# Rows of four edges, two to a partition, in the edge stage of a graph-and-mixer block

## The reference, cut to what matters

```python
xn = _layernorm(x)
e = einsum('ehd,ehd->eh', k[src], q[dst]) / 16        # 4 heads of 64
ex = exp(e - segment_max(e, dst)[dst])
a = ex / segment_sum(ex, dst)[dst]
ft2 = segment_sum(v[src] * a[..., None], dst)         # 3125 x 256
rst = layernorm(ft2 + xn); rst = layernorm(rst + ffn(rst))
x = x + rst + mixer(xn)
x = x + two_of_eight_experts(layernorm(x))
```

## Time and profile before

| | us |
|---|---|
| median of 3 runs | 2857.79 (2846.66 to 2863.58) |
| span of the profiled execution | 2291.0 |
| what lies around the span (median less span) | 566.8 |
| project stage | 0 to 118 |
| edge stage, with the second mixer | 118 to 1443 |
| merge stage | 1443 to 1585 |
| feed-forward part and experts | 1585 to 2291 |

### The profile page before, as it was taken

The page is one execution under the profiler, slowest core; times in us unless marked ns, Lnnn a source line. Parts: engine busy times, 40 slices in busy tenths (PEclk is TensorE's granted clock), DMA queues, the critical chain, the costliest instruction groups (busy, mean ns, idle before and its releaser), DMA issues. The chain is left out here.

```text
span 2291.0 us, 44322 instructions
## 1 busy us (share of the span) xinstructions
PE 1830.8 (80%) x12285; PEld 1291.9 (56%) x12285; DVE 1833.5 (80%) x3705; ACT 1525.4 (67%) x5228; POOL 1257.2 (55%) x1281
## 2 busy tenths in 40 slices
PE   7767788887786688787888771487999679999996
PEld 4433333333333566666666650244988579999995
DVE  7389999999999999999999999555899854444442
ACT  2267777778877587887888875687555255555553
POOL 0177777777777577777777776375000024444442
PEclk9879999889987688988989985698999789999998
DMA  8577777777777677777878787474001282222223
GB/s 229 182 230 232 231 230 235 233 224 228 228 226 228 182 230 239 235 234 237 237 232 242 226 243 211 138 206 119 15 29 32 89 280 38 35 35 36 37 37 77
DMA packets 213272, 394.34 MB, mean 172 GB/s; under 512 B 46354, under 2 KB 140637, under 8 KB 213005
## 3 DMA queue, kind: packets, MB, share of 16 engines
q0 software_dynamic: 91392, 278.99, 43.0%
q1 hardware_dynamic: 96848, 90.41, 13.3%
q10 hardware_dynamic: 24829, 22.64, 3.0%
HBM read 346.47 MB, written 48.65 MB: 172 GB/s over the span
## 5 line engine op out<-in xcount | busy, mean ns | idle before, releaser
L804 POOL DMA_INDIRECT ring<-kv_tab,idx x1008 | 981.0, 973 | 441.0 <-issue 297.6
L1132 ACT ACTIVATE act_val<-ring,act_val 128x64 f32<-128x64 f32 x2016 | 559.2, 398 | 51.0 <-DVE part L910 46.6
L855 DVE TENSOR_TENSOR prod<-ring,tile_bank 128x1024 f32<-128x1024 f32 x252 | 299.4, 1211 | 11.2 <-ACT tile_bank L1121 6.3
L862 DVE TENSOR_REDUCE score<-prod 128x16 f32<-128x1024 f32 x252 | 298.3, 1207 | 0.0
L2149 POOL DMA_INDIRECT x_sum<-e_yw,to_row x56 | 125.0, 2232 | 218.5 <-DVE e_yw L2175 197.2
L2134 POOL DMA_INDIRECT xr<-rows,from_row x56 | 57.6, 1029 | 291.2 <-issue 290.9
L2224 PE MATMUL e_h<-e_xT,e_now 128*128 128x128 f32 x1792 | 211.7, 277 | 0.8 <-DVE e_now L2165 0.8
L2224 PEld LDWEIGHTS e_h<-e_xT,e_now 128*128 128x128 f32 x1792 | 206.9, 194 | 1.3 <-DVE e_now L2165 1.2
L2239 PE MATMUL e_yps<-e_now,e_hT 128*128 128x256 f32 x896 | 202.5, 379 | 0.0
L2189 ACT ACTIVATE e_now<-e_w_all 128x2048 f32 x56 | 106.9, 1912 | 131.2 <-PE e_yps L2239 131.2
L2239 PEld LDWEIGHTS e_yps<-e_now,e_hT 128*128 128x128 f32 x896 | 166.2, 190 | 20.1
(11 more groups left out here) (425 smaller groups left out, 4794.0 us busy)
## 6 DMA issues: line engine op xcount, KB each, us to landing
loaded<-parts SPq DMA_DIRECT2D x150, 130.0 KB, 2.3
e_w_all<-L_ffn_W SPq DMA_DIRECT2D x16, 1024.0 KB, 12.2
parts<-part ACTq DMA_DIRECT2D x126, 130.0 KB
q_win<-q_tab SPq DMA_DIRECT2D x126, 128.0 KB
ring<-kv_tab,idx POOLq DMA_INDIRECT x1008
kv_tab<-kv_t SPq DMA_DIRECT2D x25, 224.0 KB
xn_buf<-x SPq DMA_DIRECT2D x25, 125.0 KB
x_sum<-x_buf SPq DMA_DIRECT2D x25, 125.0 KB
```

The lines of the kernel that those rows point to most:

```text
L804: pool.indirect_dma_start(out=ring[:, n % RING, e, :], out_offset=None, in_=t.kv_tab, in_offset=bass.IndirectOffsetOnAxis(ap=idx[n % 6][:, ...
L855: dve.tensor_tensor(prod[half][:, :, :], ring[:, n % RING, at, 0:F], bcast(q_ps[n % 2].unsqueeze(1), 128, L // 2, F), ALU.mult).then_inc(q ...
L862: dve.tensor_reduce(score[:, at, :], prod[half][:, :, :].rearrange("p s (h d) -> p s h d", h=HG), AX.X, ALU.add).then_inc(reduced, 1)
L1132: one = act.activation(act_val[n % 2][:, h, 0:DG, e - L // 2], ring[:, n % RING, e, F + h * DG:F + (h + 1) * DG], ACT.Copy, scale=act_val[ ...
```

## The change

A row now has 4 edges (`L` = 4) and a partition holds two rows (`G` = 2), so that a tile is 256 rows with the same 8 gathers of 128; `TILES` becomes 113 and `N_STEPS` 137. Row group 0 is weighed by DVE, group 1 by ACT. `times_q` multiplies in place, into the key half of `ring`. `weigh` of tile n-1 moves to the head of tile n, between the two `times_q`. ACT writes its weighted values beside DVE's, and the four additions become two of 1040 and 520 elements. `compare` has 256 columns and stands one step earlier; its form is now that of an operation on two tensors. Queries are fetched twice (one matmul and one load of 128 KB for each group), table rows too (four transfers per tile in place of two). Their PSUM buffers are single now. `find` and `settle` are cut in two. A sixteenth of the micro steps is doubled up (`micros`), since there are fewer tiles. In the mixer's key half the values' matmuls of two heads are issued next to each other, the products with ones are dropped, and their sums come from a product of the keys with themselves (`gram_sums`) instead. The merge loads 260 KB per step, scales one group on POOL and the other on DVE, makes one matrix on ACT and the other on DVE, and issues two matmuls per step.

```diff
-L = 8
+L = 4
+G = 2
-TILES = -(-(NB - 1 + N) // 128)
+TILES = -(-(NB - 1 + N) // (128 * G))
+EXTRA = 16
+def micros(n, c):
+    i = 4 * n + c
+    return range(i + i // EXTRA, i + 1 + (i + 1) // EXTRA)
...
 # POOL: gathers
-                for e in range(L):
+                for g in range(G):
+                    wait(pool, (val_ready, act_val_ready)[g], n - RING + 1)
+                    for e in range(L):
...
 # DVE, edge stage
+                dve.scalar_tensor_tensor(later[n % 2][:, :, :], place[:, :, :], float(128 * G * n),
+                                         bcast(blocks[n % NBUF][:, :, 2 * T3C:].bitcast(F32), 128, G, 128), ALU.add, ALU.is_ge)
...
+                k = ring[:, n % RING, g * L:(g + 1) * L, 0:F]
+                dve.tensor_tensor(k, k, bcast(q_ps[g].unsqueeze(1), 128, L, F), ALU.mult).then_inc(q_read[g], 1)
...
             def fold(n):
                 dve.wait_ge(val_ready, n + 1)
-                dve.wait_ge(exp_ready, n + 1)
-                dve.tensor_tensor(v[:, 0:2, :], v[:, 0:2, :], v[:, 2:4, :], ALU.add).then_inc(folding, 1)
+                dve.wait_ge(act_val_ready, n + 1)
+                dve.tensor_tensor(v[:, :, 0:2 * FD], v[:, :, 0:2 * FD], v[:, :, 2 * FD:], ALU.add).then_inc(folding, 1)
...
+                dve.tensor_tensor(part[n % 2][:, :, :], v[:, :, 0:FD], v[:, :, FD:2 * FD], ALU.add).then_inc(folded, 1)
...
-            def sum_act(n):
-            def fold_last(n):
...
 # DVE's order in tile n: times_q 0, weigh n-1, times_q 1, add_up 0 and 1, keep_own, compare n+5, top, less_top, fold n-1, fold_on n-1
...
 # PE
+            def q_of_rows(n, g):
+                wait(pe, q_read[g], n)
+                if g == 0:
+                    wait(pe, val_ready, n - 1)
+                pe.matmul(q_ps[g], spread[n % NBUF][:, g, :], q_win[n % 2][:, g, :], start=True, stop=True)
...
-                    pe.matmul(normT_ps[beyond, :], one_col[:, 1 - half:1 - half + DM], phi_k[h % 2], ...)
+                        for head in (h, h + 1):
+                            pe.matmul(gT_ps[half][at, :], v1[u % 2][:, head, 1:V1], phi_k[head % 2], ...)
...
 # merge
             for n in range(N_STEPS):
-                pe.matmul(step_ps[n % 3][:, 0:FD], hot[n % 4][:, :], scaled[n % 3][:, :], start=True, stop=True)
+                pe.matmul(step_ps[n % 3][:, 0:FD], hot0[n % 4][:, :], scaled0[n % 3][:, :], start=True, stop=False)
+                pe.matmul(step_ps[n % 3][:, 0:FD], hot1[n % 4][:, :], scaled1[n % 3][:, :], start=False, stop=True)
...
+            for n in range(N_STEPS):          # DVE
+                if n + 1 < N_STEPS:
+                    mark(n + 1)               # tensor_scalar, iota against local
+                    scale(n + 1)              # tensor_tensor, loaded by weights
                 dve.tensor_tensor(at, at, step_ps[n % 3][:, 0:FD], ALU.add)
...
 # load_blocks
-    sp.dma_start(to[1:128, :], ...); sp.dma_start(to[0:1, :], ...)
+    for g in range(G):
+        sp.dma_start(to[1:128, g, :], ...); sp.dma_start(to[0:1, g, :], ...)
```

More of the change, by code:

```diff
@@ L68 @@
 Q_MICRO = COEF_MICRO + KEEP + 2
+EXTRA = 16
 HW = HM // 2 * V1
+FD = HG * (DG + 1)
+FAR = 60000.0
 NEX = 8
@@ L1038, in mix @@
                         onto_x(NT - 1)
+            def mix(n, c, stretch):
+                *whole, last = micros(n, c)
+                if stretch == 0:
+                    for i in whole:
+                        for part_of in range(3):
+                            mix_step(i, part_of)
+                mix_step(last, stretch)
             dve.memset(x.k_factor[:, :], SCALE)
@@ L1067, in _ @@
                     times_q(n, 0)
+                if old:
+                    weigh(n - 1)
                 mix(n, 0, 1)
@@ L1081, in _ @@
                     keep_own(n)
-                if old:
-                    weigh(n - 1)
+                if n + AHEAD + 1 < TILES:
+                    compare(n + AHEAD + 1)
                 if now:
@@ L1214, in _, with find_rows @@
+                    if c == 1 and n + AHEAD < TILES:
+                        settle_rows(n + AHEAD)
+            for j in range(2):
+                act.wait_ge(part_out[j], 16 * len(range(j, TILES, 2)))
         @block.tensor
         def _(pe):
-            def find(n):
+            def find_rows(n):
                 pe.wait_ge(compared, n + 1)
-                wait(pe, find_read, n)
-                pe.matmul(where_ps[n % 2], later[n % 2][:, :], blocks[n % NBUF][:, 0:T3C], start=True, stop=False)
-                pe.matmul(where_ps[n % 2], later[n % 2][:, :], blocks[n % NBUF][:, T3C:2 * T3C], start=False, stop=True)
-                pe.matmul(local_ps[n % 2], beside[:, :], later[n % 2][:, :], start=True, stop=False)
-                pe.matmul(local_ps[n % 2], off_by[:, 0, :], off_by[:, 1, :], start=False, stop=True).then_inc(found, 1)
@@ L1224, in q_of_rows, with find_nodes @@
-            def q_of_rows(n):
-                pe.wait_ge(q_in[n % 3], 16 * (n // 3 + 1))
+                wait(pe, where_read, n)
+                for g in range(G):
+                    for part_of in (slice(0, T3C), slice(T3C, 2 * T3C)):
+                        mm = pe.matmul(where_ps[:, g, :], later[n % 2][:, g, :], blocks[n % NBUF][:, g, part_of], start=(part_of.start == 0),
+                                       stop=(part_of.start > 0))
+                mm.then_inc(found, 1)
+            def find_nodes(n):
+                wait(pe, gap_ready, n)
+                pe.matmul(local_ps, beside[:, :], later[n % 2][:, :, :], start=True, stop=False)
+                pe.matmul(local_ps, off_one[:, :], off_row[:, :, :], start=False, stop=True).then_inc(local_found, 1)
@@ L1248, in sums, with gram_sums @@
                 mm.then_inc(slv_ready, 1)
+            def gram_sums(u, half):
+                at = slice(half * 128, (half + 1) * 128)
+                pe.matmul(gram_ps[:, half, :], k_.unit[u % 2][:, at], k_.unit[u % 2][:, at], start=False, stop=(u == NT - 1),
+                          skip_group_check=True)
             def k_first(u, k):
@@ L1285, in coef @@
                         mm.then_inc(g_turned, 1)
+                    pe.wait_ge(g_kept, 2 + HM // 2)
+                    for half in range(2):
+                        for b in range(NPB):
+                            mm = pe.matmul(pair_sum_ps[half][:, :, b, :], x.pair4[:, b * PB:(b + 1) * PB],
+                                           gram[:, half, :].rearrange("p (h d) -> p h d", h=HM // 2), start=True, stop=True)
+                    mm.then_inc(g_turned, 1)
                 elif 0 <= h < HM:
```

610 lines of the change are left out of this document (325 added, 285 removed).

## The result

The changed kernel takes 2727.31 us (median of 5, 2705.75 to 2732.58), the kernel before in the same session 2857.79 us (median of 5, 2846.66 to 2863.58): a ratio of 0.953 [0.949, 0.957], 130 us faster.

A forecast was written before the change was run, and what follows sets the result against it. DVE was taken to bound the edge stage, with POOL's gathers close behind, and ACT the merge steps. Project +6, edge -140, merge head +9 and steps +49 gave -76: 2782 us, range 2725 to 2850.

The forecast's parts named there:

- As do the 567 us around the span: Whole kernel: the 567 us between profiled span and median time were counted as lying outside the span and unchanged.
- DVE's 9.9 us a tile: Edge stage: DVE's work per tile was to fall from 10.53 to 9.9 us.
- I take 0.4 per tile, a third of the way: Edge stage, query half: tighter waits and PE work add 0.4 us, giving 55 tiles of 10.55 us.
- PE as the bound of the query half: Rival, query half: PE sets tiles of 11.4 us, 47 us more, total -29, 2829 us; chance 0.2.
- GpSimd's floor of 10.0 to 10.15: Edge stage: eight gathers per tile hold a tile at 10.0 to 10.15 us, above DVE's 9.9.
- Project +6: Project stage: SP's two more transfers for each of five first tiles cost +6 us (0 to +12).
- Merge head +9: Head of the merge: longer scans, doubled copies and exponential, more transposes and matmuls cost +9 us (6 to 12).
- Merge steps +49: Merge steps: 137 steps at 1.2 us, 164 us in place of 115, +49 (bounds +26 to +90).
- A ceiling of 0.80 for the DMA engines: Rival, edge stage and merge steps: DMA engines can't be busier than now; +57, 2915 us; chance 0.1.
- The better case: Rival, edge stage and merge: POOL's floor and a cheap merge, -137, 2721 us; chance 0.17 with all beyond -105.
- The pair of value matmuls, nothing: Mixer's key half: issuing two heads' value matmuls next to each other is worth nothing by itself.
- The rival with 113 tiles of the old length: Rival, edge stage: fold waits for ACT, tiles stay at 10.53 us but 13 fewer, total -60; no separate chance.

The follow-up runs named there:

- x3c_both: Both edits, weights in two SBUF buffers and fold a tile later, against the changed kernel; this run fell on a quick chip: 2346.88 us, ratio 1.024.
- the late fold: Changed kernel with the fold of a tile taken one tile later; alone, on a slow chip: 2718.75 us, ratio 0.955.

## Why the prediction was wrong

**The frame of the sum.** "As do the 567 us around the span" is the first step that failed. Spans are 1.8 to 2.2 us shorter than the times in every run here; nothing lies around them. The profiled execution was one of 2291 us on a quick chip, and the 567 us were stops of PE, and ScalarE's waits for it, inside the very stage that the change rebuilds. They are fewer in the changed kernel: ScalarE's waits went from 620 to some 430 us. That, and not the shorter work counted in the forecast, is why the result is faster. On a quick chip, where the trace was taken that the terms rest on, their -76 came out at +56; the sign of the result was right for a reason that the prediction didn't have, and so was 2727 at the lower end of its 2725 to 2850: luck.

**DVE's 9.9 us a tile:** right, 9.94.

**"I take 0.4 per tile, a third of the way":** the term of the edge stage that was mis-sized. The waits were named in the right places (the fold for ACT's last weighing, queries in one PSUM buffer that tie PE to DVE), but priced in the query half alone and at a third. Measured on a quick chip, tiles are 11.36 apart in the key half (forecast 10.15) and 11.57 in the query half (10.55): 1.2 and 1.0 more. Over the 53 and 52 intervals seen there this makes 53 x 1.21 + 52 x 1.02 = 117 us, and the seven tiles around the coefficients took 103 us where the forecast's 36 + 4 x 10.35 are 77: 143 us together, what lies between 1179 and 1322. The rival nearest to it, PE as the bound of the query half, had -29 for the whole: it missed that the same ring closes in the key half.

**GpSimd's floor of 10.0 to 10.15:** right for a gather of 0.95 to 0.97, but a gather's length depends on what DVE does: 1.01 in the changed kernel, 1.14 with both edits. The long gathers were read as the comparison's doing. But the long one of the earlier trace rows had begun inside the old fold, and from 0.09 us behind its start to the fold's end are 0.49: 0.95 + 0.49 = 1.44, and 1.41 is read.

```profile
421.58 0.68 DVE L892 TENSOR_TENSOR val<-val 128x520 f32<-128x520 f32 x1
```

By what the prediction drew from the Trainium skill ("VectorE: DVE Perf Modes"), a comparison with two tensor inputs would make them go; instead 33 of the 44 gathers that began beside the new one were longer, 4 of 16 beside the old: what matters is where the operands lie. So that agreement of page and trace was none.

**Project +6:** +12 to +16, the upper end of its range. **Merge head +9:** +7. **Merge steps +49:** +44 to +46, at 160 us against 164. **A ceiling of 0.80 for the DMA engines:** the steps ran at 0.81 on a quick chip, and 100 us of the edge stage at 0.83 (1180 to 1280), so there is none at 0.80; the edge stage as a whole stood at 0.75. That this rival's +57 is nearly the +56 of the quick chip is chance: it had 1300 for the edge stage and 176 for the steps, where 1322 and 160 were measured. (The better case adds 12 us for project stage and head where the sum has 15; nothing hangs on these 3 us.) **The pair of value matmuls, nothing:** right.

**The rival with 113 tiles of the old length** came nearest in its mechanism (the fold waits for ACT), yet the tile is longer than before, not as long: 10.50 to 11.67 us eats all of the 13 tiles saved.

What stays open: what stops PE on the slow chips, and so why the changed kernel loses less there. The stops shrink with the gathers (a quarter fewer, and 440 us of stops become 119), but no run separates their number from the bytes, and none says whether the stops are there when nothing is recorded: the slow traces also lack many signals (of some 2210 that DVE gives in the edge stage of the kernel before, about 1070, against one on a quick chip). That ACT's issuing of the transfers stops ACT itself, the idea behind the run with the transfer moved to SP, is not what the late signals of PE look like; that run didn't fall on a slow chip.

## What to carry to other kernels

Before a span is subtracted from a median, run the kernel once more: a gap of 567 us meant another condition, not work outside the span, and an edit can win in one and lose in the other (0.956 and 1.024). Before an engine is said to stand still, look when the signal that it waits for was given, and not only when the operation before it ended. A saving on the busiest engine counts only down to the next ring of waits: follow one tile round from the buffer that is no longer double (here the weights in the queries' PSUM bank) to the operation that now has nothing ahead of it to hide behind (`fold`). And where GpSimd issues gathers, count its time by where the operands of DVE's operations beside it lie.

## What the runs showed of the hardware

**A gather waits for a DVE operation that reads two operands from SBUF.** Timeline of DVE and POOL, changed kernel, quick chip:

```profile
512.31 1.24 DVE L919 TENSOR_TENSOR val<-val 128x1040 f32<-128x1040 f32 x1 [1.32 <-ACT val L1158]
513.02 1.35 POOL L826 DMA_INDIRECT ring<-kv_tab,idx  x1 [0.30 <-issue]
...
514.54 1.21 DVE L882 TENSOR_TENSOR ring<-ring,tile_bank 128x1024 f32<-128x1024 f32 x1
514.68 0.95 POOL L826 DMA_INDIRECT ring<-kv_tab,idx  x1 [0.31 <-issue]
```

The first gather starts within the fold, which ends at 513.55: 0.95 + 0.44 (from 0.09 us behind its start to there) = 1.39, and 1.35 is read. The second starts in a product whose other operand is in PSUM, and takes 0.95. The same with the weights in SBUF (`x3c_both`):

```profile
533.52 1.22 DVE L911 TENSOR_TENSOR val<-ring,w_of 128x1024 f32<-128x1024 f32 x1
534.06 1.50 POOL L826 DMA_INDIRECT ring<-kv_tab,idx  x1 [0.30 <-issue]
```

Over that whole run (`x3c_both`), 322 of the 345 gathers of over 1.0 us are 0.95 us and what was left of DVE's operation 0.09 us behind their start, within 0.06. By the operation met there: `weigh` with SBUF weights lengthened 94 of 102 by 0.52 on average, the fold 95 of 101, the second fold 110 of 110; the product with q in PSUM none of 172, the sum of scores (one SBUF operand) none of 101. In the changed kernel `weigh` with its weights in PSUM lengthened none of 106. So both edits cost GpSimd what they gave. Its gathers are 120 us longer in all (1033.6 against 913.4); `weigh` with SBUF weights makes up 94 x 0.52 = 49 of it, and the second fold, which the late fold put where gathers run, some 110 x 0.57 = 62 (in the changed kernel it met 15).

The Trainium skill ("SBUF — State Buffer", shared port pair) says that a DVE operation with two SBUF inputs excludes a GpSimd operation that reads SBUF; the trace agrees, with 322 of 345, if the gather's read of its row numbers is that read. The same page of the Trainium skill has DVE's `tensor_tensor` leave GpSimd's DMAs alone; for these gathers the measurement says otherwise.

**In the merge steps the exclusion isn't complete.** Of DVE's 137 scales with two SBUF operands, 89 lie wholly outside GpSimd's; of the two wholly inside one, one takes 0.86 us, but the other 0.41, no longer than alone. The mark takes 0.28 us beside nothing of GpSimd's and up to 0.72 beside its scale (changed kernel, quick chip):

```profile
1562.77 0.62 POOL L1607 TENSOR_TENSOR scaled<-g_ring,m_weights 128x260 f32<-128x260 f32 x1 [0.81 <-DMA g_ring<-parts]
1562.82 0.65 DVE L1669 TENSOR_SCALAR hot<-iota,local 128x125 f32<-128x125 f32 x1 [1.06 <-issue]
1563.39 0.41 DVE L1664 TENSOR_TENSOR scaled<-g_ring,m_weights 128x260 f32<-128x260 f32 x1
```

**Chips differ by a quarter of the time** for one program (the kernel before, 2291 us on three chips and 2855 on a fourth), all of it in the stage with the gathers; its other stages agree within 2 us. On the slow one PE stands idle there for 373 us without a wait that the profile shows, on a quick one for none.
